# Two layers on one core: work moved across the borders of the attention, and both ends of the scan layer rearranged

## What is computed

```
xc, z = split(fc1(x) @ in_proj.T)
u = silu(sum(xc shifted by w * conv_w[:, w] for w in 0..3) + conv_b)
dt_low, B, C = split(u @ x_proj.T);   dt = softplus(dt_low @ dt_proj.T + b)
h[t] = exp(dt[t] * A) * h[t-1] + dt[t] * u[t] * B[t];   y[t] = sum(h[t] * C[t])
s = fc2((y + u * D) * silu(z) @ out_proj.T);   g = silu(down(silu(gate(x)) * up(x)))
```

## Time and profile before

| | us |
|---|---|
| median of 3 runs (2848.01 to 2854.64) | 2851.25 |
| the profiled execution, its own time | 2858.88 |
| its span, first to last instruction | 2857.1 |
| prepare, to the first product of the attention | 285.5 |
| attention, to the first transfer of the scatter | 558.0 |
| scatter, to the first transfer of layer 1 | 49.8 |
| layer 1 | 1963.8 |

### The profile page before, as it was taken

The page is one execution under the profiler, slowest core; times in us unless marked ns, Lnnn a source line. Parts: engine busy times, 40 slices in busy tenths (PEclk is TensorE's granted clock), DMA queues, the critical chain, the costliest instruction groups (busy, mean ns, idle before and its releaser), DMA issues. The chain is left out here.

```text
span 2857.1 us, 37061 instructions
## 1 busy us (share of the span) xinstructions
PE 2544.6 (89%) x13290; PEld 1481.0 (52%) x13290; DVE 2307.1 (81%) x2865; ACT 2024.1 (71%) x3261; POOL 2058.5 (72%) x680
## 2 busy tenths in 40 slices
PE   6886779999967699999999999999999999999978
PEld 2443233444424356656566565665655656656555
DVE  6675567777823598998989989899899898998985
ACT  3322356666643697887878879788798797988864
POOL 0556101111121699999999999999999999999996
PEclk9998789999988799999999999999999999999989
DMA  6247959999532321313213123032130321312210
GB/s 180 94 132 190 284 131 235 219 234 241 162 110 70 126 104 38 127 46 111 104 38 127 63 93 125 17 127 88 68 127 29 118 99 53 126 41 109 105 37 8
DMA packets 129488, 323.84 MB, mean 113 GB/s; under 512 B 15741, under 2 KB 84349, under 8 KB 112782
## 3 DMA queue, kind: packets, MB, share of 16 engines
q1 hardware_dynamic: 107034, 249.05, 28.4%
q0 software_dynamic: 19968, 71.38, 8.1%
q10 hardware_dynamic: 2304, 1.05, 0.2%
HBM read 286.75 MB, written 43.13 MB: 115 GB/s over the span
## 5 line engine op out<-in xcount | busy, mean ns | idle before, releaser
L1474 DVE TENSOR_TENSOR_SCAN l_st<-l_p_a,l_hl,l_st 128x512 f32<-128x512 f32 x768 | 932.4, 1265 | 106.8 <-ACT l_p_a L1733 97.7
L1655 POOL TENSOR_TENSOR l_st<-l_st,l_cs 128x2048 f32<-128x2048 f32 x192 | 871.0, 4560 | 0.0
L1733 ACT ACTIVATE l_p_a<-l_dt,lw_a_neg 128x512 f32<-128x512 f32 x1024 | 664.6, 680 | 44.9 <-DVE keep_xg L1474 36.9
L1647 POOL TENSOR_TENSOR l_st<-l_bs,l_dtu 128x2048 f32<-128x2048 f32 x128 | 583.7, 4560 | 32.1 <-PE l_p_y L2004 29.8
L2004 PEld LDWEIGHTS l_p_y<-keep_ident,l_st 128*128 128x128 f32 x3072 | 358.6, 146 | 141.9 <-POOL l_st L1655 72.9
L2004 PE MATMUL l_p_y<-keep_ident,l_st 128*128 128x128 f32 x3072 | 388.1, 283 | 45.4 <-POOL l_st L1655 45.2
L989 ACT ACTIVATE a_pr<-a_p_s 128x512 f32<-128x512 f32 x512 | 284.9, 596 | 168.7 <-PE a_p_s L1052 164.9
L903 DVE TENSOR_REDUCE a_mpart<-a_p_m 128x1 f32<-128x512 f32 x512 | 311.4, 681 | 8.9 <-PE a_p_m L1014 8.0
L1474 DVE TENSOR_TENSOR_SCAN keep_xg<-l_p_a,l_hl,keep_xg 128x512 f32<-128x512 f32 x256 | 314.7, 1266 | 1.9 <-issue 0.4
L1655 POOL TENSOR_TENSOR keep_xg<-keep_xg,l_cs 128x2048 f32<-128x2048 f32 x64 | 292.5, 4570 | 2.0 <-ACT l_hl L1738 2.0
L835 POOL DMA_DIRECT2D a_w<-in_w_dram x32 | 23.1, 725 | 351.0 <-PE a_p_m L1080 294.3
(11 more groups left out here) (232 smaller groups left out, 3961.5 us busy)
## 6 DMA issues: line engine op xcount, KB each, us to landing
l_bs<-s_bc SPq DMA_DIRECT2D x64, 1024.0 KB, 4.7
l_cs<-s_bc SPq DMA_DIRECT2D x64, 1024.0 KB, 4.8
a_w<-in_w_dram POOLq DMA_DIRECT2D x32, 1024.0 KB, 11.9
late<-in_w_dram POOLq DMA_DIRECT2D x32, 1024.0 KB, 19.2
kx<-s_kp SPq DMA_DIRECT2D x96, 256.0 KB, 12.7
keep_share<-s_x SPq DMA_DIRECT2D x32, 512.0 KB, 4.9
s_kp<-late SPq DMA_DIRECT2D x96, 128.0 KB, 2.1
s_vp<-late SPq DMA_DIRECT2D x16, 544.0 KB, 3.3
```

The source lines that it names most:

```text
L1474: eng.tensor_tensor_scan(st[k % NG][:, n, :], p_a[:, n, :], st[k % NG][:, n, :], hl[:, k, n:n + 1], ALU.mult, ALU.add).then_inc(scan_ok, 1)
L1647: eng.tensor_tensor(st[n][:, :, :], bs[:, 4 * n:4 * n + 4, :], dtu[(k // NG) % 2][:, :].unsqueeze(1).broadcast_to([P, NG, TT]), ALU.mult). ...
L1655: eng.tensor_tensor(st[n][:, :, :], st[n][:, :, :], cs[:, 4 * n:4 * n + 4, :], ALU.mult).then_inc(cm_ok, 1)
L1733: eng.activation(p_a[:, n, :], dt[c % 2][:, :], ACT.Exp, scale=a_neg[:, c, m:m + 1]).then_inc(dA_ok, 1)
```

## The change

Nothing is computed that was not computed before; work changes its place, its engine or its order.

1. Prepare: SP's loop ends at `NT`, so the keys of tiles 14 and 15 are stored by SP in the attention, behind the loads of pass 1. ACT issues its query stores one tile earlier.
2. Attention: at g = 1 DVE waits for `b1` alone; the picked rows are marked four passes later than before, so that the wait for the three other transfers comes at g = 4, and four of them stand at the end. POOL asks for `w1` of quad 1 before `w2` of quad 0. The copies of x leave the passes and come behind them in SP's list, released by the progress of passes 11 to 15. `outputs` of quad 6 moves from pass 15 to pass 14, that of quad 7 from chunk 3 to chunk 5 of pass 15.
3. Scatter: the bias of `Wo` is waited for by PE and by the second round of DVE, not by its first instruction. ACT turns the int32 weights here, one after each of `folded_in` 1 to 3, and DVE makes the diagonals here. `folded_out` leaves.
4. Layer 1, start: PE folds the output weights first; ACT loads one function table up front, and again ahead of `project`; the four convolutions of tile 0 are done by DVE into PSUM; `norm_scale(1)` comes later.
5. Layer 1, end: the last `weighed` goes from POOL to DVE, the last residual from POOL to DVE in two halves, each stored by itself; PE sums slots 14 and 15 ahead of `down(0)`, and `back(3)` comes ahead of `down(1)`.

```diff
@@ prepare, SP and ACT
-                for t in range(NT + 2):
+                for t in range(NT):
                     if t >= 2:
                         keys_out(t - 2)
...
-                    if t == NT:
-                        group_queries()
+                group_queries()
...
-                    if t in (13, 14):
-                        store_queries(eng, t - 12)
+                    if t in (12, 13):
+                        store_queries(eng, t - 11)
@@ attention, SP
-                    if hg % 2:
-                        half = bass.ds(b * S + hg // 2 * (S // 2), S // 2)
-                        eng.dma_start(scr["x1"][half, :].rearrange("(p a) d -> p (a d)", p=P),
-                                      ins["x"][half, :].rearrange("(p a) d -> p (a d)", p=P)).then_inc(x1_out, 16)
+                    if g == 1:
+                        keys_out(NT - 2)
+                        keys_out(NT - 1)
+
+                def copy_x(i):
+                    eng.wait_ge(pv_ok, 8 * 12 + 4 * i)
...
                 passes(eng, load)
+                for i in range(2 * B):
+                    copy_x(i)
                 eng.wait_ge(x1_out, 16 * 2 * B)
@@ attention, POOL
                 load_first(0)
+                load_first(1)
                 load_second(0)
-                load_first(1)
@@ attention, DVE, ACT and PE
+                        if i == 26 and g == G - 1:
+                            experts_out(QUADS - 2)
...
                         if g == 1:
-                            eng.wait_ge(consts, 16 * 4)
+                            eng.wait_ge(consts, 16)
...
-                    one_choice(*prev(g, b, hg))
+                    if g == HG:
+                        eng.wait_ge(consts, 16 * 4)
+                    if g >= HG:
+                        one_choice(g - HG, b - 1, hg)
...
-                    one_choice(G - 1, B - 1, HG - 1)
+                    for hg in range(HG):
+                        one_choice(G - HG + hg, B - 1, hg)
...
-                    wait(eng, eo_out, (q - 1) * 64)
+                    wait(eng, eo_out, (q if q == QUADS - 1 else q - 1) * 64)
...
-                        if c == 3 and g == G - 1:
+                        if c == 4 and g == G - 2:
+                            outputs(QUADS - 2)
+                        if c == 5 and g == G - 1:
                             outputs(QUADS - 1)
@@ scatter
+                def whole_weights(n):
+                    eng.wait_ge(lw_in, 16 * N_LW)
+                    eng.activation(lw[n][:, :, :].bitcast(F32), lw[n][:, :, :], ACT.Copy)
...
                     if 3 <= k < 7:
                         folded_in(k - 3)
+                    if 4 <= k < 7:
+                        whole_weights(("g_int", "u_int", "d_int")[k - 4])
                 folded_bias()
-                for h in two:
-                    folded_out(h)
@@ layer 1
+                def first_conv(c):
+                    bank_free(eng, 0, "cv", c)
+                    taken(eng, "xc", 0, c)
+                    sum_c = p_w[:, bank("cv", c), :]
+                    eng.tensor_scalar(sum_c, xc[c % 2][:, 0:TT], conv_w[:, c, 0:1], None, ALU.mult).then_inc(tap_ok, 1)
+                    for k in range(1, 4):
+                        eng.wait_ge(tap_ok, 3 * c + k)
+                        eng.scalar_tensor_tensor(sum_c, xc[c % 2][:, k:k + TT], conv_w[:, c, k:k + 1], sum_c, ALU.mult, ALU.add)\
+                           .then_inc(tap_ok if k < 3 else full["cv"], 1)
...
+                def last_weighed():
+                    eng.wait_ge(hl_ok, NT * SLOTS)
+                    eng.wait_ge(c_in_ok[NG - 1], NT * 16)
+                    eng.tensor_tensor(st[NG - 1][:, :, :], st[NG - 1][:, :, :], cs[:, NST - 4:NST, :], ALU.mult).then_inc(cm_last, 1)
+
+                def last_residual(h):
+                    eng.wait_ge(old_in, NT * 16)
+                    taken(eng, "op", NT - 1, h)
+                    half = slice(2 * h, 2 * h + 2)
+                    eng.tensor_tensor(gate[:, half, :], gate[:, half, :], xt[:, half, :], ALU.add).then_inc(res_ok, 1)
...
+                eng.preload_act_table_set("natural_log_exp_and_others")
                 eng.activation(a_exp[:, :, :], a_exp[:, :, :], ACT.Exp).then_inc(a_ok, 1)
-                eng.activation(w_g[:, :, :], g_int[:, :, :], ACT.Copy)
-                eng.activation(w_u[:, :, :], u_int[:, :, :], ACT.Copy)
-                eng.activation(w_d[:, :, :], d_int[:, :, :], ACT.Copy).then_inc(a_ok, 1)
```

More of the change, by code:

```diff
@@ L1183, in heads, with diagonals @@
                                       ALU.mult).then_inc(on_ok, 1)
+                def diagonals(c):
+                    for w in range(4):
+                        eng.tensor_scalar(lw["cdiag"][:, c * 4 + w, :], ident[:, :], lw["conv_w"][:, c, w:w + 1], None, ALU.mult)
+                    eng.tensor_scalar(lw["sdiag"][:, c, :], ident[:, :], lw["skip"][:, c:c + 1], None, ALU.mult)
                 def rows(k):
@@ L1250, in folded_bias @@
                     m.then_inc(made, 1)
-                def folded_out(h):
-                    if h == 0:
-                        eng.wait_ge(out_in, 16 * 2)
-                    eng.wait_ge(copied, 4 + h)
-                    for c in (2 * h, 2 * h + 1):
-                        for k in range(KD):
-                            m = eng.matmul(p_w[1 - h][:, (c % 2) * D:(c % 2 + 1) * D], outp[:, k, c * P:(c + 1) * P], fc2_t[:, k, :],
-                                           start=k == 0, stop=k == KD - 1)
-                    m.then_inc(made, 1)
                 def turn(k):
@@ L1580, in period @@
                         scan_unit(s, 7, 0)
+                    if q == 0:
+                        for c in range(CB):
+                            first_conv(c)
                     if nxt:
@@ L1684, in period @@
                         dbu(s, 1)
-                    if end:
+                    if end and f < NT - 1:
                         weighed(f, 15)
@@ L1826, in period @@
                         normed(q)
+                    if q == 0:
+                        folded_out(0)
+                        folded_out(1)
                     if scan:
@@ L1974, in period @@
                         last(s, 14)
+                    if q == 0:
+                        norm_scale(1)
                     if front:
@@ L1992, in _ @@
             def _(eng):
-                eng.wait_ge(diag_ok, 1)
-                eng.wait_ge(a_ok, 2)
+                eng.wait_ge(set_ok, 1)
+                for h in two:
+                    for c in (2 * h, 2 * h + 1):
+                        for k in range(KD):
+                            i = eng.matmul((p_y, p_u)[h][:, (c % 2) * D:(c % 2 + 1) * D], outp[:, k, c * P:(c + 1) * P], fc2_t[:, k, :],
+                                           start=k == 0, stop=k == KD - 1)
+                    i.then_inc(fold_ok, 1)
                 def sums(t, k):
@@ L2095, in period @@
                         turn(q, q, 1)
-                    if end:
+                    if end and q <= NT:
                         sums(f, 15)
@@ L2100, in period @@
                         conv_in(q, q, p, 1)
+                    if end and q <= NT:
+                        down(q, f, 1)
                     if end:
+                        back(q, f, p, 3)
+                    if q == NT + 1:
                         down(q, f, 1)
-                        back(q, f, p, 3)
                     if scan:
```

117 lines of the change are left out of this document (80 added, 37 removed).

## The result

The changed kernel takes 2819.98 us (median of 4, 2818.44 to 2824.28), the kernel before beside it 2850.93; ratio 0.9884, 95% interval 0.9873 to 0.9896. That is 31 us less, 13 short of the 44.6 forecast.

What follows compares the result with a forecast made beforehand. Layer 1 was taken as bound by POOL once its scans run, leaving borders, ends and idle times to gain: -6.5 - 25 - 8 + 0 - 7.8 + 2.7 = -44.6, from 2851.25 to about 2807 us; 8 in 10 range 2788 to 2826.

Steps and rivals of the forecast that it cites:

- the likeliest case: Whole kernel: all terms inside their bounds, about 2807 us, own range 2796 to 2818; chance 0.61.
- Border, -6.5: Prepare to attention: moving 14 stores into the attention starts PE at 279 instead of 285.47; -6.5 us (-3 to -13).
- Stall, -25: Attention, g = 1: DVE waits for `b1` alone, so the 54.37 us pass loses its stall; -25 us (-15 to -26).
- Rival D: Attention, g = 1: DVE still held by something landing when `rank` did, pass stays at 54; 2832 us, chance 0.04.
- Rival A: Passes 2 to 4: late keys or values make PE wait 10 to 22 us; 2817 to 2829, chance 0.15.
- End of the attention, -8: Pass 15: earlier `w2` of quad 7 saves 10, last copy of x costs 2; -8 us (-10 to -1).
- rival C: End of the attention: copies of x pile up and hold the stage; slower, about 2948 us, chance 0.03.
- Scatter, 0: Scatter stage: an earlier end and added conversions cancel; 0 us (-1 to +2).
- The two halves: Scatter: dropping `folded_out` gives about 3 us; three conversions on ACT's row path take 4.2.
- Start of layer 1, -7.8: Layer 1's start: four table loads leave the path, 5.1, and convolutions on DVE give 2.7; -7.8 us (-4.5 to -12).
- the 2.7 for them: Layer 1's start: gain from convolutions on DVE, taken between 1.1 (PE at half clock) and 6.2 (full clock).
- End of layer 1, +2.7: Layer 1's end: DVE's last `weighed` waits for POOL's whole instruction, delaying PE's last `up` by 3.6; +2.7 us (-2 to +6).

Runs made afterwards that it cites:

- u6: Changed kernel with the last 14 key stores (tiles 14 and 15) back in prepare; 2827.74 us, ratio 0.9913.
- b2: Kernel before with only `w1` of quad 1 issued ahead of `w2` of quad 0, DVE still waiting for `rank` at g = 1; 2831.15 us, ratio 0.9926.
- b1: Kernel before with DVE waiting at g = 1 for `b1` only and picked rows marked four passes later; 2833.89 us, ratio 0.9934.
- u1: Changed kernel with DVE at g = 1 waiting for all four transfers again; 2822.64 us, ratio 0.9894.
- u2: Changed kernel with `outputs` of quad 6 back in pass 15, its waits, copy out and store with it; 2819.88 us, ratio 0.9884.
- s1: Changed kernel with the three integer weight conversions behind the eight scatter rounds on ACT; 2817.08 us, ratio 0.9872.
- u4: Changed kernel with the last `weighed` still on DVE but behind two of the three last `hidden`; 2813.79 us, ratio 0.9863.
- v1: Changed kernel with last `weighed` behind two `hidden`, conversions behind the rounds, and tile 0's convolutions on PE again; 2809.35 us, ratio 0.9843.
- b3: Kernel before with only the eight copies of x moved behind the passes; 2854.49 us, ratio 1.0007.
- u9: Changed kernel with DVE waiting at g = 1 for all four transfers and `w2` of quad 0 ahead of `w1` of quad 1; 2847.67 us, ratio 0.9977.

## Why the prediction was right, and where it was not

The direction and the range were right, 2819.98 in 2788 to 2826, but at its upper end, outside the likeliest case's own range.

- **Border, -6.5.** -6.8 from PE's last product of prepare on, -6.0 by u6. In the nine profiles with this border PE starts 2.5 to 2.6 behind the landing of tile 13's store, where I took 2. That the store decides is likely and not shown: SP's program waits only for the loads issued behind it, whose landing the traces don't list. Before, SP's issuing set the start, by the same kind of reading: the issue of its last store ends at 284.97, and PE starts 0.5 later, as in all five profiles with the old border. The stage table's -9.5 holds 2.7 that prepare was earlier in this one execution.
- **Stall, -25.** The size was right, -24.9 in the profiles; the step "Its cause stands in the same rows", that DVE sits there until `rank` has landed, was only half of it. The order of `w1` and `w2`, which I named only as what comes late next, removes the stall alone (b2), as the wait does (b1). I had added one gain for two edits that each bring it, and so the sum was right with the attribution unfinished. Rival D, that the edit at g = 1 wouldn't do it, falls by b1; but beside the new order of loads that edit is worth nothing that can be told (u1). Rival A, late data in the passes, is refuted: passes 2 and 3 take 29.88 and 30.21. Passes 2 to 13 together are 1.7 longer than before, for a reason not looked into.
- **End of the attention, -8.** This step failed. From L967 of pass 14 (L993 now) to the last take it is 72.14 before and 69.32 after, -2.8. "`outputs` of quad 6 now comes a pass earlier" was costed at nothing, as if its 3.64 only left one pass and entered another. In the old place it stood in the hole that ACT's gelu makes, and hid; in pass 14 it is 3.6 on PE's path, and the open hole of 3.14 is followed by half clock, 4.17 a chunk where 2.88 is usual, three times: 3.9. Together 7.5, near the 7.2 that are missing from -10. u2 shows both. The copies of x, for which I took 2, cost nothing: they land 5.1 to 13.5 after their issue, the last one at 799.4, 7.9 ahead of the last take, and rival C, the slower side, had no ground.
- **Scatter, 0.** +0.8. The two halves were right: the conversions lay on the path with 4.1 (s1).
- **Start of layer 1, -7.8.** -6.1 to the first `dtu`, -7.5 from the second `dtu` on (7.5 to 9.2 later). The table loads gave what I took: the two at the norm 2.7 (3.31 to 0.62 from `nmr` to `rstd`), the one in dt 1.3, and the one ahead of the first `exp_unit` 1.4 behind that `dtu`. The convolutions did not: the step that failed is the 2.7 for them, which measured 1.6 the other way (30.45 for 28.88, from the first copy of `xc` to that of `xd`). I had set the clock between two levels, where the products of `xc` 2 and 3 and `project` ran at the lower one (granted 0.50 to 0.58 while they ran) and lost 1.8, 1.8 and 2.6. The 1.1 at the lower bound doesn't follow from its rows either: two convolutions at 0.87 would give 1.7. That the sum still hit is luck: 2.0 more came ahead of the first product, and 1.8 from that product itself, which ran at full clock in this profile (3.67 for 6.29) and in no other with DVE's convolutions; in those the first `dtu` comes 49.3 to 51.3 after the stage's start, in the changed kernel's 49.0, before 55.2.
- **End of layer 1, +2.7.** +3.9, and the mechanism was right. PE's last `up` came 6.6 after the last `hl` instead of 2.8, +3.8 for 3.6; half clock and PE's other waits +2.5 for +1.1, the tail -2.5 for -2.0. u4 against the changed kernel settles that DVE's product waited for POOL's and isn't slow by itself.

Against its own profile the sum was 4 off: -44.6 for -40.5. That is less than the 7.2 missing at the end of the attention, since the earlier prepare put 2.7 on the other side, which no term of mine had. The larger part of the 13 is the base. I applied a difference of profiled executions to the median, but the profiled execution of before was 7.6 above its median and that of after 1.6 below its own (2818.44 to 2819.98). That is 9 us of scatter between executions, and the stall is a good candidate for some of it: b1 and b2 are 27 shorter in the span of their profiles and 20 and 22 in the median. How the 9 divide is open, as is a drift of 2 us in layer 1: counted from the stage's start, the changed kernel leads by 7.5 at the second `dtu` and by 9.7 at the last `hl`. The profiles of u4 and v1, with the same scans, move too, in steps of 1.2 to 1.4 and either way, so I lay nothing on it.

## What to carry to other kernels

A product that fills a hole made by another engine is free only there. Before moving it, ask which hole it stood in, and what the clock does when that hole opens. When a change holds two edits near one stall, undo each alone and both together: undoing one shows nothing if the other is enough. A wait put ahead of work that is already due costs its whole length; put behind that work, the same instruction can be free.

## What the runs showed of the hardware

- A 128x2048 f32 product on DVE with both inputs in SBUF took 2.28 us behind POOL's instruction (u4, v1) and 5.25 when asked for 3 us ahead of that instruction's end (changed kernel); POOL's 4.5 us instruction was not slowed. The listed duration holds the wait. The Trainium skill ("SBUF — State Buffer", "Who interferes with whom") gives this as an exclusive lock, and these runs agree.
- After a hole of 3.14 us in PE's work the granted clock was 0.50, its lower level of 1.2 GHz, for 12 us, though PE was busy 11.48 of them; the products of layer 1's start with 5.1 us idle ahead of each ran at half as well (granted 0.50 and 0.53 around 3.75 for 1.96, 0.58 over `project`), though 0.91 and 0.83 were granted in idle stretches between them.
- `rank`, a load of 4 KB on SP's queue, landed 33.0 us after its issue where the 4 MB of `w2` had gone out ahead of it, and 17.9 without them (b2), where its issue also came 12 us earlier. It was hardly beside them: the four loads of `w2` landed at 323.2, 326.5, 332.8 and 343.1, and `rank` went out at 334.1. So they made it late through what was queued before it; how was not tried.
- SP's six key loads of pass 3 take 18.7 us to issue before, 17.8 in b2 and 16.6 in b3, so `w2` isn't what holds them. In the changed kernel, u1 and u9 they take 2.9, and in u6, where the stores are back in prepare, 16.8: where the 14 stores stand ahead, it is the seven stores of tile 15 that take 11.2 to 11.7, against 4.7 to 5.3 for those of tile 14. The hold stays and moves to what is issued there. What causes it wasn't tried.
